# A two-layer transformer block whose layer and expert loops are written out: constant counts and addresses in place of registers and jumps

## The chip, the cores and the metric

The kernel runs on one core of one Trainium2 chip. The metric is the device time in microseconds of one execution. The kernel before takes 2094.49 us, the median of 3 runs (2094.24 to 2097.22).

## What is computed

Two layers on x of 2 sequences of 2048 tokens with 256 features, in float32. Each layer normalizes, scales and shifts x by rows made from a conditioning vector, applies a mixer, adds it back through a gate, and does the same with a feed-forward part.

- Layer 0's mixer is gated linear attention in chunks of 64 (4 heads, keys of 128, values of 64); its feed-forward part is 64 small one-input networks.
- Layer 1's mixer is a state-space scan: for 512 channels and 16 states, one step per token,

```
dtv = sigmoid(dt_t + dt_head_b)
dtv = dtv / (1 + dtv * sum(k_t * k_t))
state = state * (1 - dtv * k_t * k_t) + (x_t * dtv) * k_t
y_t = sum over the states of state * q_t
```

- Layer 1's feed-forward part is 8 experts, each of which takes the 512 tokens of a sequence that score highest for it:

```
g, m = top_k(softmax(x @ gate_w), 512)
h = gelu(x[m] @ w1[e]) @ w2[e]
out[m] += g * h
```

## The kernel before, in words

The program is written by hand: each engine (PE, DVE, ACT, POOL, and SP for the DMA queue) has its own list of instructions, and they meet at semaphores, whose counts only go up. An engine's sequencer reads the list, does register work, jumps and DMA issues itself, and hands the rest to the engine behind it.

**The layers** cut the 4096 tokens into NB = 16 blocks of 256. A block passes through five stages (A attention, F the rest up to the scan's inputs, S scan, C what comes after the scan, G gate scores), and in turn i the stages work on blocks i+2, i+1, i, i-1 and i-2. A turn is 64 steps; the table `AT` says at which step each piece is put into its engine's list. `pipeline` writes the turns: -1 to 2 written out, 3 to 13 as a loop (11 passes), 14 to 18 written out again. So turns 2 and 14 are the same Python code as the loop's body, with a constant in place of the register: turn 2 has no stage G yet, and turn 14 no longer loads a block of x. Each engine has a loop of its own and jumps back on its own; nothing joins the engines at the jump.

The scan's pieces are what the turn is full of. For each of the 16 states, SP reads that state's k and q rows back from memory, broadcast over 128 partitions, into one of 4 slots of `kqb` (`spread`, L1262 to L1264); POOL makes the input, `st = u * k` (L1090); DVE scans in place (L1071, four instructions per state) with decays that ACT makes (L1052) and PE turns (L1022); POOL reads out, `sq = st * q` (L1080), and PE adds the turned result up in PSUM (L1039). POOL's list puts the input of state m+3 between the read-outs of states m and m+1, and adds small pieces of the four layer norms (L466 to L469). A slot of `kqb` is loaded again once its state is read out:

```
sp.wait_ge(sem("read_out"), it * DS + n - SLOTS + 1)
both = kq_d[bass.ds(it % 2, 1)].rearrange("o (w n) t -> o n w t", w=2)[:, n]
sp.dma_start(kqb[:, n % SLOTS], both.broadcast_to([P, 2, TB])).then_inc(sem(f"kq_in{n % SLOTS}"), 16)
```

In a turn SP's list is: `kqb` of states 4 to 9, the output rows (L1276), the normalized rows for the experts (L1279), the next load of x (L1256), `kqb` of states 10 to 15, then for the next block the k and q rows (L1289), `ndT` (L1293) and `kqb` of states 0 to 3. DVE's list has, near its start, two halves of `ndS` (L993), scans, the gated `lz` (L769) and the two halves of `u` (L999), the scan input of the next block.

In the loop, a count such as `it * DS + n - 3` and an address such as block `it % 2` are made from the loop's register by the sequencer (a register instruction, shown by the profile as ALU_OP, FUSED_REGOPS or MOVE) ahead of the instruction that uses it. In the turns that are written out they are constants in the instruction.

**The experts** are 16 lists (8 experts, 2 sequences) after the choice of tokens. `every_turn` loops over three turns of 4 lists (2 experts) and writes the fourth out, with less in it, since nothing is prepared for a next one. Per list PE multiplies in split precision (L1750: `ph`, 8 pieces; `po`, 4 pieces), ACT applies gelu and copies, DVE splits values (L1590, L1593) and scales (L1632), POOL gathers and scatters rows; POOL's part is written out already. Two short loops stand beside it: SP loads the weights of experts 1 to 7 (L1457), and ACT copies the first expert's 8 weight pieces (L1693).

Of the kernel before, what the change touches and what calls it, by code (L numbers as in the profile page):

```python
# [19 lines left out]
NB = B * T // TB  # L20
# [10 lines left out]
E, F = 8, 1024  # L31
# [132 lines left out]
def layers(nc, sem, x_rows, consts, weights, folds, wmod0, wmod1, out_rows, xn_d,  # L164
           scores, ones_s, ident_s, col1, gb1):
    with ExitStack() as ctx:
# [1130 lines left out]
        def pipeline(eng, a_turn):  # L1297

            a_turn(eng, -1, "A")
            a_turn(eng, 0, "AF")  # L1300
            a_turn(eng, 1, "AFS")
            a_turn(eng, 2, "AFSC")
            with eng.Fori(3, NB - 2) as i:
                a_turn(eng, i, "AFSCG")
            a_turn(eng, NB - 2, "AFSCG")
            a_turn(eng, NB - 1, "FSCG")
            a_turn(eng, NB, "SCG")
            a_turn(eng, NB + 1, "CG")
            a_turn(eng, NB + 2, "G")

        with nc.Block() as block:
            @block.sync
            def _(sp):
                pipeline(sp, turn_sp)
                sp.wait_ge(sem("x_out"), (NB + 1) * 16)
                sp.wait_ge(sem("rows_out"), (NB + 1) * 16)

            @block.tensor
            def _(pe):
                pipeline(pe, turn_pe)  # L1320

            @block.scalar
            def _(act):
                act.preload_act_table_set("natural_log_exp_and_others")
                act.wait_ge(sem("tail0"), 2)
                pipeline(act, turn_act)
# [18 lines left out]
def experts(nc, sem, consts, w1_d, w2_d, out_rows, xn_d, scores, ones_s, ident_s, col1, gb1):  # L1345
    with ExitStack() as ctx:
# [16 lines left out]
        WQ = 2 * DC * F // K  # L1363
# [48 lines left out]
        def flat(x):  # L1412
            return x.rearrange("p a b -> p (a b)")
# [5 lines left out]
        ITEMS = NL // 4  # L1419
# [8 lines left out]
        def splits(i, n, ahead):  # L1428

            no_weights = WQ // 2 if n == 3 and not ahead else 0  # L1430
            return FIRST + (i - 1) * 4 * PER_LIST + n * PER_LIST - no_weights

        def ring(n, more):

            return (FIRST + n * PER_LIST + more) % 4

        def every_turn(eng, a_turn):
            with eng.Fori(1, ITEMS) as i:
                a_turn(eng, i, True)
            a_turn(eng, ITEMS, False)  # L1440

        with nc.Block() as block:
            @block.sync
            def _(sp):
                def load(e):
                    for n, w_d in enumerate((w1_d, w2_d)):
                        sp.dma_start(w_in[:, n].rearrange("p (c f) -> p c f", c=w_d.shape[1] // P),
                                     w_d[bass.ds(e, 1)].rearrange("e (c p) f -> p (e c) f", p=P))\
                            .then_inc(sem("w_in"), 16)

                for name, dst in (("bitsf", bitsf[:, :]), ("samelist", samelist[:, :]),
                                  ("segbefore", segbefore[:, :]), ("iota", iota[:, :]),
                                  ("token", token[:, :, :].rearrange("p a n -> p (a n)"))):
                    a, n = CONST_AT[name]
                    sp.dma_start(dst, consts[:, a:a + n]).then_inc(sem("const2_in"), 16)
                load(0)
                with sp.Fori(1, E) as e:  # L1457

                    sp.wait_ge(sem("w_split"), e * WQ)
                    load(e)  # L1460

            @block.vector
            def _(dve):
# [145 lines left out]
                def a_turn(dve, i, ahead):  # L1609
                    for n in range(4):  # L1610
# [34 lines left out]
                        if n % 2 == 1 and ahead:  # L1645
                            for c in range(2):
                                slots_of(i * 4 + n - 1 + c, c)

                every_turn(dve, a_turn)

            @block.scalar
            def _(act):
                act.wait_ge(sem("sel_step"), 2)
                act.activation(prob[:, :, :].rearrange("p t e -> p (t e)"), scores[:, :], ACT.Exp)\
                    .then_inc(sem("prob_exp"), 1)

                def put(to, count, at_ring):

                    act.wait_ge(sem("masked"), count)
                    act.activation(to, masked[:, at_ring, :], ACT.Copy).then_inc(sem("upper"), 1)  # L1660

                def put_weights(slot, q, count, at_ring):
                    n, at = q // 4, (q % 4) * K
                    put(w_up[:, slot, n, at:at + K], count, at_ring)

                def modulated(k_count, b):
                    for c in range(DC):
                        act.wait_ge(sem("gt_mm"), k_count + c + 1)
                        sc, sh = ((what * DC + c) * B + b for what in (4, 3))
                        act.activation(hg[:, c, :], pt[:, c, :], ACT.Identity, bias=col1[:, sh:sh + 1],  # L1670
                                       scale=col1[:, sc:sc + 1]).then_inc(sem("hg"), 1)

                def a_turn(act, i, ahead):
                    for n in range(4):
                        for f in range(FT):
                            act.wait_ge(sem("up_mm"), i * 4 * FT + n * FT + f + 1)

                            act.wait_ge(sem("h1_split"), i * 4 * FT + n * FT + f - 3)
                            act.activation(h1[:, f % 4, :], ph[:, f % 2, :], ACT.Gelu).then_inc(sem("gelu"), 1)  # L1679
                            if f > 0:  # L1680
                                put(h1_up[:, f - 1, :], splits(i, n, ahead) + f, ring(n, f - 1))
                        put(h1_up[:, FT - 1, :], splits(i, n, ahead) + FT, ring(n, FT - 1))
                        if ahead or n < 3:

                            modulated((i * 4 + n + 1) * DC, (n + 1) % 2)
                            for c in range(DC):
                                put(hg_up[:, c, :], splits(i, n, ahead) + FT + c + 1, ring(n, FT + c))
                        if ahead or n < 2:
                            for q in range(WQ // 2):
                                put_weights(1 - n // 2, n % 2 * (WQ // 2) + q, splits(i, n, ahead) + FT + DC + q + 1,  # L1690
                                            ring(n, FT + DC + q))

                with act.Fori(0, WQ) as q:  # L1693
                    act.wait_ge(sem("masked"), q + 1)
                    act.activation(flat(w_up[:, 0])[:, bass.ds(q * K, K)], flat(masked[:, :, :])[:, bass.ds(q * K, K)],
                                   ACT.Copy).then_inc(sem("upper"), 1)
                modulated(PER_TURN["gt_mm"], 0)
                for c in range(DC):
                    put(hg_up[:, c, :], WQ + c + 1, (WQ + c) % 4)
                every_turn(act, a_turn)  # L1700

            @block.tensor
            def _(pe):
# [50 lines left out]
                def a_turn(pe, i, ahead):  # L1754
                    for n in range(4):
# [24 lines left out]
                        if ahead and n % 2 == 1:  # L1780
                            for c in range(2):
                                slots_of(i * 4 + n - 1 + c, c)

                every_turn(pe, a_turn)

            @block.gpsimd
# [98 lines left out]
```

## Time and profile before

| what | value |
|---|---|
| time, median of 3 runs | 2094.49 us |
| the profiled execution's own time | 2097.58 us |
| its span, first to last instruction | 2095.4 us |
| PE busy | 1771.5 us (85%), 12344 matmuls |
| DVE busy | 1569.0 us (75%) |
| ACT busy | 1301.9 us (62%) |
| POOL busy | 1439.5 us (69%) |
| DMA | 132.78 MB, mean 63 GB/s |
| mean granted TensorE clock | 0.934 of full speed |

How to read it: times are in us from the span's first instruction. PE is the matmul part of TensorE and PEld its weight loads; DVE is VectorE, ACT ScalarE, POOL GpSimd, SP the engine that issues most DMAs. A name with q (POOLq) is the engine's sequencer, whose register work, jumps and issues are not counted as busy. A view by windows gives for each stretch its length, then busy time and instructions of each engine, the granted clock, the DMA engines' busy share and GB/s. A view of waits gives who waited for whom: us in total, times, longest. In a timeline the number in brackets is the engine's idle time just before, and what ended it; "issue" there is a time in which it waited for nothing that the profile shows. The view of one source line gives the count and then minimum, median and maximum of the duration in ns, and the first and last start.

### The profile page before, as it was taken

What the parts mean: (1) busy time and instruction counts of PE and PEld (TensorE: products, weight loads), DVE (VectorE), ACT (ScalarE), POOL (GpSimd) and SP (SyncE); (2) the same over time, 40 slices, a digit from 0 to 9 for tenths busy, and PEclk for the clock granted to TensorE, in tenths of its full rate; (3) what the DMA queues carried; (4) which work ended last, traced back from release to release, by engine and by line L of the source; (5) the groups of instructions that cost most, each with busy time, mean ns of one, the idle gap of its engine ahead of it and who ended that gap; (6) DMA issues with size and microseconds to landing.
All of it is one profiled execution on the core that took longest, in us unless ns stands there. A gap on an engine that the chain in (4) does not pass through costs nothing. (4 is left out here: it accounts for less than half of the span.)

```text
span 2095.4 us, 40115 instructions
## 1 busy us (share of the span) xinstructions
PE 1771.5 (85%) x12344; PEld 1521.1 (73%) x12344; DVE 1569.0 (75%) x3158; ACT 1301.9 (62%) x2316; POOL 1439.5 (69%) x836
## 2 busy tenths in 40 slices
PE   5578998989989899898998989988662499999996
PEld 5456887877878778787887878876551388888886
DVE  3336898887978888888888888987646777777772
ACT  0257787776867777777777777876321255555552
POOL 0005899998989989899898999999970244343342
PEclk9788999999999999999999999999875599999998
DMA  4001332223223233322322222223211233333321
GB/s 167 15 1 47 68 67 60 65 58 76 62 56 64 59 75 56 64 65 57 76 55 65 63 59 76 60 64 61 69 39 57 71 79 81 77 81 75 76 45 21
DMA packets 110368, 132.78 MB, mean 63 GB/s; under 512 B 7969, under 2 KB 103073, under 8 KB 109985
## 3 DMA queue, kind: packets, MB, share of 16 engines
q1 hardware_dynamic: 97680, 113.04, 22.3%
q0 software_dynamic: 12288, 16.79, 4.4%
q10 hardware_dynamic: 272, 1.57, 0.2%
q8 instruction: 41, 0.67, 0.1%
q14 instruction: 87, 0.70, 0.1%
HBM read 105.68 MB, written 17.30 MB: 59 GB/s over the span
## 5 line engine op out<-in xcount | busy, mean ns | idle before, releaser
L1071 DVE TENSOR_TENSOR_SCAN st<-pD,last,st 128x256 f32<-128x256 f32 x1024 | 693.9, 732 | 136.3 <-PE pD L1022 114.3
L1090 POOL TENSOR_TENSOR st<-u,kqb 128x1024 f32<-128x1024 f32 x256 | 605.0, 2363 | 85.2 <-DMA kqb<-kq_rows 76.1
L1080 POOL TENSOR_TENSOR sq<-st,kqb 128x1024 f32<-128x1024 f32 x256 | 605.0, 2363 | 26.9 <-DVE st L1071 22.5
L1052 ACT ACTIVATE decT<-ndT,ones_s,kkT 128x512 f32 (+1 forms) x512 | 407.4, 806 | 81.5 <-PE pD L1022 72.6
L1039 PE MATMUL pY<-ident_s,sq 128*128 128x128 f32 x2048 | 324.6, 283 | 62.1 <-POOL sq L1080 62.0
L1022 PE MATMUL pD<-ident_s,decT 128*128 128x128 f32 x2048 | 326.2, 284 | 53.7 <-DVE st L1071 48.3
L1022 PEld LDWEIGHTS pD<-ident_s,decT 128*128 128x128 f32 x2048 | 251.3, 146 | 108.8 <-DVE st L1071 61.6
L1039 PEld LDWEIGHTS pY<-ident_s,sq 128*128 128x128 f32 x2048 | 247.3, 145 | 81.8 <-POOL sq L1080 77.5
L1805 POOL DMA_INDIRECT y_out<-ys,ids x64 | 108.6, 1698 | 247.1 <-DVE ys L1632 150.4
L1750 PE MATMUL po<-w_up,h_up 128*128 128x256 f32 x512 | 147.8, 289 | 19.9 <-DVE h_rest L1593 19.0
L1750 PE MATMUL po<-w_rest,h_up 128*128 128x256 f32 x512 | 145.5, 284 | 0.0
L1750 PE MATMUL po<-w_up,h_rest 128*128 128x256 f32 x512 | 145.4, 284 | 0.0
L1794 POOL DMA_INDIRECT xg<-xn_rows,ids x64 | 69.3, 1083 | 91.6 <-DVE gates L1581 72.4
L1679 ACT ACTIVATE h<-ph 128x512 f32<-128x512 f32 x128 | 76.6, 598 | 76.5 <-PE ph L1750 73.5
L621 PE MATMUL pA<-hA,W 128*128 128x256 f32 x512 | 118.5, 379 | 0.8 <-DVE qg L708 0.8
L1750 PEld LDWEIGHTS po<-w_up,h_up 128*128 128x128 f32 x512 | 98.7, 193 | 25.1 <-issue 17.0
L1750 PE MATMUL ph<-hg_up,w_up 128*128 128x512 f32 x256 | 103.7, 405 | 8.9 <-DVE w_rest L1593 6.4
L466 POOL TENSOR_TENSOR nm_a<-mv_a,minus 128x2 f32<-128x2 f32 x16 | 3.1, 195 | 155.5 <-DVE ve_a L461 154.2
L621 PEld LDWEIGHTS pA<-hA,W 128*128 128x128 f32 x512 | 94.8, 190 | 19.2 <-issue 7.2
L1750 PE MATMUL ph<-hg_up,w_rest 128*128 128x512 f32 x256 | 102.7, 401 | 0.0
L1750 PE MATMUL ph<-hg_rest,w_up 128*128 128x512 f32 x256 | 102.7, 401 | 0.0
L1750 PEld LDWEIGHTS po<-w_up,h_rest 128*128 128x128 f32 x512 | 98.9, 193 | 0.0
(269 smaller groups left out, 3756.3 us busy)
## 6 DMA issues: line engine op xcount, KB each, us to landing
kqb<-kq_rows SPq DMA_DIRECT2D x256, 256.0 KB, 4.6
w_in<-w_d SPq DMA_DIRECT2D x16, 1024.0 KB
ndT<-ndS SPq DMA_DIRECT2D x16, 512.0 KB, 3.4
xt<-x_in SPq DMA_DIRECT2D x16, 256.0 KB, 2.8
y_out<-xo SPq DMA_DIRECT2D x16, 256.0 KB, 4.8
xn_rows<-xnC SPq DMA_DIRECT2D x16, 256.0 KB, 2.1
W<-weights SPq DMA_DIRECT2D x1, 3505.5 KB, 21.9
wmod<-wmod ACTq DMA_DIRECT2D x1, 1536.0 KB, 11.0
```

The costliest lines, as they stand in the source:

```text
L466: pool.tensor_tensor(nm[n][:, :], mv[n][:, :, 0], minus[:, :], ALU.mult)
L621: i = pe.matmul(bank[:, h2 * TB:(h2 + 1) * TB], wt[:, c, h * DK:(h + 1) * DK], hA[:, c, :], start=(c == 0), stop=(c == DC - 1))
L1022: i = pe.transpose(pD[h][:, k2 * TB + t * P:k2 * TB + (t + 1) * P], decT[:, m % 2, t, (2 * h + k2) * P:(2 * h + k2 + 1) * P], ident_s[:, :])
L1039: i = pe.matmul(pY[:, t, k * P:(k + 1) * P], sq[:, m % 2, k, t * P:(t + 1) * P], ident_s[:, :], start=False, stop=(m == DS - 1), is_transp ...
L1052: act.activation(decT[:, m % 2, t, :], turn2(ndT, it, NT * DI, t * DI, DI), ACT.Identity, bias=ones_s[:, 0:1], scale=turn2(kkT, it, NT * D ...
L1071: dve.tensor_tensor_scan(run, pD[h][:, k2 * TB:(k2 + 1) * TB], run, last[:, bass.ds(later(it) * (DS * DT) + m * DT + k, 1)], ALU.mult, ALU ...
L1080: pool.tensor_tensor(sq[:, m % 2], st[:, m % 4], kqb[:, m % SLOTS, 1, :].unsqueeze(1).broadcast_to([P, DT, TB]), ALU.mult).then_inc(sem("r ...
L1090: pool.tensor_tensor(st[:, m % 4], turn2(u, it, DT * TB).rearrange("p (k t) -> p k t", k=DT), kqb[:, m % SLOTS, 0, :].unsqueeze(1).broadca ...
L1679: act.activation(h1[:, f % 4, :], ph[:, f % 2, :], ACT.Gelu).then_inc(sem("gelu"), 1)
L1750: m = pe.matmul(to, stationary(c, p0), moving(c, p1), start=(n == 0), stop=(n == len(terms) - 1))
L1794: pool.indirect_dma_start(xg[:, b, s, :], None, xn_d[:, :], bass.IndirectOffsetOnAxis(ap=ids[:, k * SL + s:k * SL + s + 1], axis=0))\
L1805: pool.indirect_dma_start(out_rows, bass.IndirectOffsetOnAxis(ap=ids[:, k * SL + s:k * SL + s + 1], axis=0), ys[:, b, s, :], None, compute ...
```

## The change

Four loops over a register become Python loops, so that their bodies stand in the lists once per pass: the layers' turns 3 to 13 on all five engines, the experts' turns 1 to 3 on PE, ACT and DVE, SP's loads of expert weights 1 to 7, and ACT's 8 copies. Counts and addresses become constants, and the jumps and the register work go. The work, its order and its waits stay.

```diff
@@ -1300,7 +1300,7 @@
             a_turn(eng, 0, "AF")
             a_turn(eng, 1, "AFS")
             a_turn(eng, 2, "AFSC")
-            with eng.Fori(3, NB - 2) as i:
+            for i in range(3, NB - 2):
                 a_turn(eng, i, "AFSCG")
             a_turn(eng, NB - 2, "AFSCG")
             a_turn(eng, NB - 1, "FSCG")
@@ -1435,7 +1435,7 @@
         def every_turn(eng, a_turn):
-            with eng.Fori(1, ITEMS) as i:
+            for i in range(1, ITEMS):
                 a_turn(eng, i, True)
             a_turn(eng, ITEMS, False)
@@ -1454,7 +1454,7 @@
                 load(0)
-                with sp.Fori(1, E) as e:
+                for e in range(1, E):
 
                     sp.wait_ge(sem("w_split"), e * WQ)
                     load(e)
@@ -1690,7 +1690,7 @@
-                with act.Fori(0, WQ) as q:
+                for q in range(WQ):
                     act.wait_ge(sem("masked"), q + 1)
```

DVE's list near the start of a turn, in the loop before. ISA and REGISTER_ALU are the sequencer's register instructions; L999 makes `u`, the scan input of the next block.

```order
L768 REGISTER_ALU
L769 TENSOR_TENSOR lz<-pA,sg 128x512
L997 ISA
L998 ISA
L999 ISA
L999 TENSOR_TENSOR u<-pB,xs 128x512
L997 REGISTER_ALU
L999 ISA
```

The same place in the list of the change:

```order
L769 TENSOR_TENSOR lz<-pA,sg 128x512
L999 TENSOR_TENSOR u<-pB,xs 128x512 x2
L1071 SCALAR_TENSOR_TENSOR st<-pD,last,st 128x256 x2
L773 TENSOR_TENSOR og<-pA,lz 128x512
L453 BN_STATS stat_a<-xt 128x6 x2
```

The register instructions are gone, six in the piece shown, and the engine's own instructions stand as they stood.

SP's list in the middle of a turn, in the loop before: the two output DMAs, the load of x, and the first `kqb` load behind them.

```order
L1276 DMA y_out<-xo 128x2x256
L1279 DMA xn_rows<-xnC 128x2x256
L1282 ISA
L1256 ISA x2
L1256 DMA xt<-x_in 128x2x256
L1262 REGISTER_ALU
L1264 ISA
L1264 DMA kqb<-kq_rows 128x2x256
```

The same place in the list of the change:

```order
L1264 DMA kqb<-kq_rows 128x2x256 x10
L1276 DMA y_out<-xo 128x2x256
L1279 DMA xn_rows<-xnC 128x2x256
L1256 DMA xt<-x_in 128x2x256
L1264 DMA kqb<-kq_rows 128x2x256 x6
```

Here too only the register rows have gone: three ahead of the load of x and two ahead of each `kqb` load.

## Rows read from the trace of the kernel before

**Rows 1.** Busy time by windows, the layers (PE, PEld, DVE, ACT, POOL, clock, DMA):

```profile
150.00:1565.00 1415.00, 1264.38 (x9137) 1075.78 (x9137) 1158.88 (x2246) 1024.77 (x1843) 1256.15 (x689) 0.96 0.28 62
```

**Rows 2.** The layers' loop line: the jumps on POOL's and DVE's sequencer:

```profile
L1303 POOLq COMPARE_BRANCH  x11: 40/45/45, 401.0 to 1280.3; - x11
L1303 DVEq COMPARE_BRANCH  x11: 55/63/72, 418.5 to 1297.5; - x11
```

**Rows 3.** POOL by windows (POOL, clock, DMA): turns 3-13, turn 2, turn 14:

```profile
318.78:1284.76 965.98, 867.57 (x485) 0.98 0.29 64
232.40:318.78 86.38, 78.88 (x46) 1.00 0.28 65
1284.76:1367.72 82.96, 78.88 (x45) 1.00 0.26 65
```

**Rows 4.** POOL's waits, us 318.78 to 1284.76, the 11 looped turns:

```profile
POOL st L1090 <- DMA kqb<-kq_rows: 59.6, 54, 4.0
POOL sq L1080 <- DVE st L1071: 18.9, 20, 1.8
POOL nm_b L466 <- DVE ve_b L461: 5.2, 9, 1.4
POOL st L1090 <- issue: 3.6, 11, 0.3
```

**Rows 5.** POOL's waits, us 1284.76 to 1367.72, turn 14, written out:

```profile
POOL st L1090 <- DMA kqb<-kq_rows: 3.1, 5, 2.0
POOL sq L1080 <- DVE st L1071: 0.2, 1, 0.2
```

**Rows 6.** POOL's waits, us 232.40 to 318.78, turn 2, written out:

```profile
POOL st L1090 <- DMA kqb<-kq_rows: 2.9, 2, 2.7
POOL sq L1080 <- PE pY L1039: 2.8, 2, 1.5
```

**Rows 7.** DVE's timeline behind the jump at the end of looped turn 9:

```profile
951.49 1.39 DVE L1071 TENSOR_TENSOR_SCAN st<-pD,last,st 128x256 f32<-128x256 f32 x2 [1.51 <-PE pD L1022]
...
955.13 1.29 DVE L999 TENSOR_TENSOR u<-pB,xs 128x512 f32 x2 [1.67 <-issue]
```

**Rows 8.** DVE's timeline at the same place of turn 14, written out:

```profile
1300.88 1.39 DVE L1071 TENSOR_TENSOR_SCAN st<-pD,last,st 128x256 f32<-128x256 f32 x2 [1.00 <-PE pD L1022]
...
1302.77 1.28 DVE L999 TENSOR_TENSOR u<-pB,xs 128x512 f32<-128x512 f32 x2
```

**Rows 9.** DVE's waits, us 318.78 to 1284.76, the 11 looped turns:

```profile
DVE u L999 <- issue: 18.7, 10, 2.3
```

**Rows 10.** DMA queues, us 934.51 to 1022.19, looped turn 10 (packets, MB, share):

```profile
q14 instruction: 5, 0.04, 0.1%
```

**Rows 11.** DMA queues, us 1284.76 to 1367.72, turn 14, written out:

```profile
q8 instruction: 4, 0.07, 0.3%
q14 instruction: 3, 0.02, 0.1%
```

**Rows 12.** SP's timeline in looped turn 10:

```profile
1011.36 0.38 SPq L1279 DMA_DIRECT2D xn_rows<-xnC  x1
1012.19 0.39 SPq L1256 DMA_DIRECT2D xt<-x_in  x1
1012.84 2.45 SPq L1264 DMA_DIRECT2D kqb<-kq_rows  x2
```

**Rows 13.** SP's timeline in turn 14, written out:

```profile
1357.60 0.39 SPq L1279 DMA_DIRECT2D xn_rows<-xnC  x1
1358.03 3.43 SPq L1264 DMA_DIRECT2D kqb<-kq_rows  x2
```

**Rows 14.** Experts by windows (all engines), lists 3, 11 (looped), 13 (written out):

```profile
1715.14:1739.95 24.81, 23.64 (x152) 21.47 (x153) 17.14 (x36) 14.05 (x24) 11.21 (x8) 1.00 0.47 128
...
1927.64:1954.08 26.44, 25.27 (x152) 22.63 (x153) 17.14 (x36) 14.05 (x24) 10.75 (x8) 0.94 0.45 119
1981.48:2006.13 24.65, 23.64 (x152) 21.44 (x153) 17.19 (x36) 14.05 (x24) 11.19 (x8) 1.00 0.46 129
```

## The prediction

> **What bounds the kernel now.** I read the windows first. From us 150 to 1565, two thirds of the time, the layers run, and POOL is busy 1256 of 1415 us; PE comes near it, but its busy time is that of overlapping records, and DVE and ACT stand at 1159 and 1025 [rows 1]. So I go to POOL and cut the layers at its own beat. The start of the input of state 11 comes once per turn, and its starts cut the stretch into the looped turns 3 to 13, which take 965.98 us, or 87.82 us each, with POOL busy for 867.57/11 = 78.87 of it [rows 3]. POOL is idle 8.95 us per turn, and only that can go: its work is the same after the change.
>
> The kernel holds its own experiment: turns 2 and 14 are the loop's body written out. Turn 14 takes 82.96 us with the same 78.88 us of POOL's work, so POOL idles 4.08 us in it; turn 2 takes 86.38 us [rows 3]. The waits say where the rest goes. Per looped turn POOL waits 59.6/11 = 5.42 us for the `kqb` loads, 18.9/11 = 1.72 for DVE's scans, 5.2/11 = 0.47 for DVE's layer-norm value, and 0.33 for nothing seen, which is its own register work in front of L1090 [rows 4]. In turn 14 it waits 3.1 us for `kqb` and 0.2 for DVE [rows 5].
>
> **What DVE is late for.** After the jump DVE idles twice in a few us: 1.51 us before a scan and 1.67 us before `u`, where it waits for no semaphore that the profile shows [rows 7]. In turn 14 the same scan has 1.00 us before it and `u` nothing [rows 8]. The wait before `u` stands in 10 of the 11 looped turns, 18.7 us in all, 1.87 each [rows 9]. It is not the jump instruction, which takes DVE 63 ns [rows 2]. The DMA queues show code being read: a looped turn has five reads on q14, though it runs the code of the turn before again, and a written-out turn has three on q14 and four on q8 [rows 10, 11]. I take `u`'s wait to be code that the jump left behind and that must be read again, with DVE's list standing still. The Trainium skill ("Runtime: NRT & Kernel Launch", section Instruction fetch mechanics) says that a taken branch to a page outside the two held forces a fetch before the engine goes on, while straight code is fetched ahead; the trace agrees, with 1.87 us behind a jump and none in turn 14. By that rule alone DVE's 11 × 1.87 = 20.6 us would be the gain, if POOL followed DVE one to one.
>
> **The change, part by part.**
>
> *The layers' loop, turns 3 to 13.* The four differences of turn 14 from a looped turn are 5.42 − 3.1 = 2.3 us of `kqb` waits, 1.72 − 0.2 = 1.5 of waits for DVE, 0.47 and 0.33: together 4.6 of the 4.86 us by which the turn is shorter; the rest lies in gaps too short for the view. The first is SP's: in the loop, register instructions stand between the read-out that frees a slot and the load's issue, and such a load lands only just in time. Where SP's list is held by the two output DMAs, 1.48 us pass from the issue of the normalized rows to the next `kqb` load, two register groups and the load of x among them [rows 12], against 0.43 us in turn 14 [rows 13].
>
> Turn 14 has no load of x, though, and the turns written out will have it. By [rows 12] its issue takes 0.39 us, with some 0.05 us to the next instruction. I add 0.45 us for that, all on the longest `kqb` wait, and 0.05 for its transfer beside the load: 83.46 us per turn. Turn 2, which has the load, shows 2.7 us for that longest wait where turn 14 shows 2.0 [rows 5, 6], so the addition lies between 0 and 0.7. The saving is 87.82 − 83.46 = 4.36 us per turn, times 11 = **48.0 us**.
>
> Bounds: turn 14 as it stands gives 4.86 × 11 = 53.5 us. Turn 2 as it stands gives 1.44 × 11 = 15.8 us. I stay near turn 14: it is full like the loop's turns and follows a full turn, while turn 2's extra 2.8 us are two waits for PE's adding-up (pY) [rows 6], in the turn where stage C appears for the first time; turn 14's waits do not have them [rows 5].
>
> *The experts' loop, 12 lists.* Here PE leads. Looped list 3 takes 24.81 us and the written-out list 13 takes 24.65, with the same work [rows 14]: 0.16 × 12 = **2 us**. From below this is 0, if the little idle time moves elsewhere. Three of the 12 looped lists meet a stretch at the lower clock (1.2 GHz); in the one shown it costs 26.44 − 24.81 = 1.63 us, at clock 0.94 over the list [rows 14]. Whether they meet it after the change I leave open: up to 4.9 us more, and as much less should others meet it.
>
> *SP's loop over expert weights and ACT's over 8 pieces* I cost at nothing: ACT's copies follow DVE's splits, and the weights are loaded a whole expert ahead. If that cover were gone, it would be some register instructions of about 0.1 us, 15 times.
>
> *Added:* nothing that computes. What comes new is PE's code: looped turn 10 has no read on q8, turn 14 has four [rows 10, 11], so 11 turns bring some 44 reads. In turn 14 they are hidden behind code already there; its POOL waits contain what they cost. If they were not hidden, see the second rival.
>
> Sum: 48.0 + 2 = 50 us from the execution that was profiled, 2097.6, gives 2047.6 us. That execution stands 3.1 us above the median of the runs, so against 2094.5 the forecast is **2044.5 us**.
>
> **Rivals.**
>
> *Only the jumps and POOL's register work go.* Then DVE's waits are of another kind, say a true dependence, and stay; so do the loads' 5.42 us. What goes is 0.33 us per turn in front of L1090 [rows 4] and 0.05 us for a jump [rows 2]: 0.38 × 11 = 4 us, and 2090 us. Against it speaks that turn 14 has neither DVE's waits nor a third of the loads'. The Trainium skill ("Advanced Engine Details and Errata", Control Flow Timing) gives about 108 ns for a compare-and-branch; by that rule alone the change would be worth 11 × 0.108 = 1.2 us on POOL, an estimate from that page. The rows have 45 and 63 ns for the jump, and most of the loss stands behind it.
>
> *Reading straight-line code costs more than the jump: slower.* A written-out turn needs seven reads where a looped one needs five, and all of PE's are new [rows 10, 11]. A read that an engine has to wait for costs about 1.87 us [rows 9]. The place would be PE's list, before a scan's decays are turned, where DVE and then POOL stand behind it. It decides from 4.36/1.87 = 2.3 exposed reads per turn; with three, a turn would be 1.25 us longer, and 11 turns 14 us: 2108 us. For it: the whole list has never been read without a pause in between, and five engines would do it at once. Against it: turn 14 does exactly this, and no wait of POOL there goes back to it [rows 5]; turn 2's waits for pY are the only ones that could [rows 6]. The Trainium skill ("Advanced Engine Details and Errata", ISA Cache) has TensorE hold 128 KB of code, four times the other engines, and only two cache lines; by this rule the loop's body can stay in PE, which agrees with no q8 read in looped turn 10, and it speaks against writing out the loop.
>
> *The `kqb` chain or PE takes over.* With DVE earlier, the start of a turn would wait as in turn 2, for PE's adding-up: 15.8 + 2 = 18 us gained, 2076.5 us. For it: turn 2 is such a turn. Against: turn 14 too, and it is steadier.
>
> **How the numbers follow.** The forecast, turns at turn 14's price with or without the load of x, gets 0.82. PE taking over 0.07, no more than the jumps 0.06, slower 0.05. The low end is 53.5 + 2 + 4.9 = 60.4 us gained, 2034, and I go to 2032 for a turn that does a little better than 14 with both neighbours written out. The high end is half way between the two written-out turns: turn 14 with its load at 83.46 and turn 2 at 86.38 make 84.9, or 2.9 × 11 = 32 us, less up to 3 for the clock: 2065.5. So the range is 2032 to 2066. A measurement of this kernel can tell 0.2%, 4.2 us, from no change. The forecast and the PE rival are faster by more, 0.89; the jump rival is within it, plus the edge of the slower one, 0.06; slower 0.05.
>
> **What would show it.** Right: turns 3 to 13 at 83 to 84 us with POOL busy 78.9; `u` without its wait for nothing; `kqb` waits near 3.5 us per turn; POOL's waits for DVE under 0.5; some 40 more reads on q8; lists of the experts at 24.65 where the clock is full. Wrong: PE's or DVE's waits for nothing that the profile shows inside turns 3 to 13, which would be code; POOL waiting for pY in every turn; or turns that keep 87 us although `u` comes early.

## The result, and the profile after

| | time, us | runs | against before |
|---|---|---|---|
| before, same chip | 2095.85 | 4 (2094.24 to 2099.12) | |
| the change | 2059.6 | 4 (2057.32 to 2060.82) | 0.9824 [0.9807, 0.9841] |

The change is faster, by 36 us; 50 were forecast. The direction and the range (2032 to 2066) hold, and the predicted 2044.5 is 15 us too low. The execution that was profiled took 2060.5 us, its span 2058.7, which is 36.7 less than before. Page of the change, parts 1, 3 and 5:

```profile
span 2058.7 us, 34361 instructions
...
PE 1756.5 (85%) x12344; PEld 1512.6 (73%) x12344; DVE 1572.4 (76%) x3158; ACT 1297.1 (63%) x2314; POOL 1440.2 (70%) x836
...
q8 instruction: 98, 1.61, 0.3%
...
q14 instruction: 71, 0.58, 0.1%
...
L1090 POOL TENSOR_TENSOR st<-u,kqb 128x1024 f32<-128x1024 f32 x256 | 605.2, 2364 | 65.1 <-DMA kqb<-kq_rows 59.0
L1080 POOL TENSOR_TENSOR sq<-st,kqb 128x1024 f32<-128x1024 f32 x256 | 605.1, 2364 | 16.7 <-PE pY L1039 11.0
```

Every engine has the work it had (ACT's count in the page is two records short of the 2316 before). 5754 instructions are gone (40115 before), all of the sequencers' own. POOL's wait ahead of its scan step L1080 is now put down to PE's adding-up `pY`; in the loop it was DVE's scan. POOL cut at the same beat as before, the start of the input of state 11, for turn 2, turns 3 to 13, and turns 14 to 16 [rows 3] (columns: window, length, POOL busy, clock, DMA share, GB/s):

```profile
232.15:319.55 87.40, 78.87 (x44) 1.00 0.27 65
```

```profile
319.55:1251.76 932.21, 867.00 (x486) 0.99 0.30 67
1251.76:1503.64 251.88, 231.92 (x122) 0.92 0.32 64
```

The same for turns 14 to 16 of the kernel before:

```profile
1284.76:1531.30 246.54, 232.00 (x122) 0.93 0.28 65
```

So the 36.7 us are: turns 3 to 13 965.98 − 932.21 = 33.8 shorter, which is 84.75 us per turn and not the 83.46 forecast; turn 2 1.0 longer (86.38 before); turns 14 to 16, whose code had been written out before, 5.3 longer; and the rest, from the first of the experts' matmuls to the end, 435.4 − 426.2 = 9.2 shorter. POOL's waits in turns 3 to 13 [rows 4]:

```profile
POOL st L1090 <- DMA kqb<-kq_rows: 42.8, 35, 4.0
POOL sq L1080 <- PE pY L1039: 5.2, 10, 1.0
POOL nm_c L466 <- DVE ve_c L461: 4.8, 8, 1.3
POOL st L1090 <- PE pY L1039: 2.8, 4, 1.0
POOL sq L1080 <- DVE st L1071: 2.5, 11, 0.5
```

Per turn: 3.89 us for `kqb` (5.42 before, 3.5 forecast), 0.23 for DVE's scans (1.72 before), nothing of its own register work (0.33). New are 8.0/11 = 0.73 us for `pY`, and 0.44 for the third layer norm's value, about what the loop lost at the second. That value is DVE's too: together POOL waits 0.66 us for DVE, where under 0.5 was forecast. DVE's timeline at the place of [rows 7, 8], end of turn 9:

```profile
927.83 1.38 DVE L1071 TENSOR_TENSOR_SCAN st<-pD,last,st 128x256 f32<-128x256 f32 x2
930.34 1.39 DVE L1071 TENSOR_TENSOR_SCAN st<-pD,last,st 128x256 f32<-128x256 f32 x2 [1.12 <-PE pD L1022]
931.65 0.67 DVE L769 TENSOR_TENSOR lz<-pA,sg 128x512 f32<-128x512 f32 x1
932.23 1.28 DVE L999 TENSOR_TENSOR u<-pB,xs 128x512 f32<-128x512 f32 x2
```

`u` starts as the step before it ends; its 1.67 us are gone. The 1.12 us ahead of the scan are PE's. POOL and PE in the same us:

```profile
927.52 2.37 POOL L1090 TENSOR_TENSOR st<-u,kqb 128x1024 f32<-128x1024 f32 x1
930.88 2.36 POOL L1080 TENSOR_TENSOR sq<-st,kqb 128x1024 f32<-128x1024 f32 x1 [1.00 <-PE pY L1039]
```

```profile
926.30 0.33 PE L598 MATMUL pA<-qg,S 128*64 128x64 f32 x2
926.47 0.28 PE L600 MATMUL pA<-att,vh 128*64 128x64 f32 x2
...
928.33 0.28 PE L598 MATMUL pA<-qg,S 128*64 128x64 f32 x2
```

From 926.3 us on PE works through 64 matmuls of the attention's output without a pause. They stand in its list ahead of a scan step's `pD` and `pY`, which follow at 929.6 and 930.1, and POOL, no longer held back by DVE, arrives before them at the read-out of state 12.

Code reads, turns 3 to 13: before, and after (queue, packets, MB, share):

```profile
q14 instruction: 57, 0.47, 0.2%
q8 instruction: 6, 0.10, 0.0%
```

```profile
q8 instruction: 52, 0.85, 0.4%
q14 instruction: 39, 0.32, 0.1%
```

On q8 there are 46 reads more, as forecast (some 40); on q14 there are fewer than in the loop, which runs the same code eleven times.

Of the experts, the 12 lists that were looped take 321.44 us before and 313.80 now. The first line of each view is all 12 together, the second is list 2, one of even number. The last two lines of the view after are list 3, of odd number and at the full clock, and list 7, which meets the lower clock (1.2 GHz) for a part of it; all engines as in [rows 14]:

```profile
1660.04:1981.48 321.44, 299.30 (x2016) 268.11 (x2017) 236.60 (x428) 172.41 (x291) 123.23 (x91) 0.97 0.30 71
1687.66:1715.14 27.48, 24.93 (x187) 22.32 (x185) 22.41 (x37) 14.04 (x24) 11.03 (x8) 1.00 0.23 39
```

```profile
1632.51:1946.31 313.80, 294.84 (x2016) 265.42 (x2017) 236.82 (x428) 169.66 (x289) 125.05 (x91) 0.99 0.32 73
1659.28:1686.32 27.04, 24.88 (x187) 22.35 (x185) 22.37 (x37) 14.05 (x24) 11.14 (x8) 1.00 0.25 40
1686.32:1710.95 24.63, 23.63 (x153) 21.45 (x153) 17.18 (x36) 14.05 (x24) 11.16 (x8) 1.00 0.48 128
1789.68:1815.93 26.25, 25.25 (x152) 22.58 (x153) 17.18 (x36) 14.05 (x24) 10.71 (x8) 0.93 0.46 121
```

A list of odd number (24.81 before) lost 0.18 us and one of even number 27.48 − 27.04 = 0.44, six of each: 3.7 us. From list 2 on, two lists fewer meet 1.2 GHz, one now for three before, at some 1.6 us each [rows 14]: 3.2 us. The 0.7 us that are left of the 7.6 belong to list 1. It meets the lower clock in both kernels, a fourth one that the forecast did not count, and takes 27.61 us before and 26.77 now. The other 1.6 us of the 9.2 lie outside these lists, nearly all in the last of the 16 (40.17 us to the end before, 38.67 now), and are not the change's: after_again, the same kernel, has 40.26 there.

### The profile page after: what moved, and what is told of

Its sections match the earlier page's. It is cut to its first block and busy times, and to the rows that moved or that the text cites. A ratio compares the mean times of both kernels' runs of the same rounds, so it can differ in the third digit from the quotient of the medians.

```text
span 2058.7 us, 34361 instructions
## 1 busy us (share of the span) xinstructions
PE 1756.5 (85%) x12344; PEld 1512.6 (73%) x12344; DVE 1572.4 (76%) x3158; ACT 1297.1 (63%) x2314; POOL 1440.2 (70%) x836
## 5 line engine op out<-in xcount | busy, mean ns | idle before, releaser
L1080 POOL TENSOR_TENSOR sq<-st,kqb 128x1024 f32<-128x1024 f32 x256 | 605.1, 2364 | 16.7 <-PE pY L1039 11.0
L1052 ACT ACTIVATE decT<-ndT,ones_s,kkT 128x512 f32<-128x512 f32 x512 | 407.0, 806 | 83.1 <-PE pD L1022 69.7
L1022 PE MATMUL pD<-ident_s,decT 128*128 128x128 f32 x2048 | 323.0, 282 | 46.7 <-DVE st L1071 40.2
L1022 PEld LDWEIGHTS pD<-ident_s,decT 128*128 128x128 f32 x2048 | 247.5, 145 | 104.8 <-issue 50.0
```

The source lines that it names most:

```text
L1022: i = pe.transpose(pD[h][:, k2 * TB + t * P:k2 * TB + (t + 1) * P], decT[:, m % 2, t, (2 * h + k2) * P:(2 * h + k2 + 1) * P], ident_s[:, :])
L1052: act.activation(decT[:, m % 2, t, :], turn2(ndT, it, NT * DI, t * DI, DI), ACT.Identity, bias=ones_s[:, 0:1], scale=turn2(kkT, it, NT * D ...
L1080: pool.tensor_tensor(sq[:, m % 2], st[:, m % 4], kqb[:, m % SLOTS, 1, :].unsqueeze(1).broadcast_to([P, DT, TB]), ALU.mult).then_inc(sem("r ...
```

## The experiments

Each kernel is given by how it differs from the change. In layers_only, registers_straight, hint, dve_only, sp_only, all_but_pe and hint_sp_pool the experts' three loops are loops again, as before; their edits show only what differs in the layers. Turn times are those of turns 3 to 13, cut as above (before 87.82, the change 84.75). The median of before moved between the groups of experiments from 2092.9 to 2095.3, so each ratio is to the runs of before that stood beside it. A turn time comes from one profiled execution, a ratio from all of them.

| kernel | median, us | ratio to before | us per turn |
|---|---|---|---|
| layers_only | 2064.28 | 0.9877 [0.9848, 0.9905] | 84.44 |
| experts_only | 2087.99 | 0.9977 [0.9960, 0.9995] | 87.31 |
| registers_straight | 2082.29 | 0.9946 [0.9929, 0.9962] | 85.52 |
| hint | 2083.92 | 0.9949 [0.9931, 0.9967] | 85.59 |
| dve_only | 2078.54 | 0.9931 [0.9910, 0.9951] | 85.60 |
| sp_only | 2087.64 | 0.9973 [0.9959, 0.9987] | 86.79 |
| all_but_pe | 2058.96 | 0.9835 [0.9821, 0.9849] | 84.42 |
| hint_sp_pool | 2071.28 | 0.9881 [0.9862, 0.9900] | 84.45 |
| after_again | 2057.96 | 0.9834 [0.9818, 0.9849] | 84.29 |
| early10 | 2050.68 | 0.9791 [0.9766, 0.9816] | 84.34 |
| nd_first | 2050.67 | 0.9808 [0.9779, 0.9837] | 84.15 |
| both | 2044.12 | 0.9765 [0.9745, 0.9785] | 84.08 |

### The two parts of the change alone

layers_only has the experts' loops back, experts_only the layers' loop; the edit is that of experts_only:

```diff
-            for i in range(3, NB - 2):
+            with eng.Fori(3, NB - 2) as i:
                 a_turn(eng, i, "AFSCG")
```

> Only the layers' loop (turns 3 to 13) is written out; the experts' turns, SP's weight loop and ACT's copies stay loops. In the changed kernel the layers up to the first expert product are 27.5 us shorter (1660.0 to 1632.5) and the experts 9.2 us shorter. Theory A (the two parts add): 2094.5 - 27.5 = about 2068 us. Theory B (the experts' 9 us are an accident of where the clock falls, or come from the layers): 2059 to 2061 us.

> The layers' loop stays a loop; the experts' turns 1 to 3, SP's weight loop and ACT's copies are written out. Theory A: lists 2, 4 and so on go from 27.5 to 27.0 us and the odd ones from 24.8 to 24.6, which is 12 x 0.3 = 3.6 us, and the rest of the 9 us is that fewer lists meet the lower clock: 2086 to 2091 us, depending on the clock. Theory B (nothing of it comes from this loop): 2094 to 2097 us.

The median of before beside them is 2094.38. The layers alone give 30 us by medians (26 by the ratio), the experts alone 6 (5). By medians that is together the change's 36; by the ratios it is 31, with intervals of 6 and 4 us to either side. In layers_only a turn takes 84.44 us and POOL's waits are those of the change. In experts_only a turn keeps 87.31 us and `u` its wait (18.4 us in all); its even lists take 27.05 us, its odd ones 24.64, and one of the twelve 26.27. The experts' term is real, and larger than the 2 us forecast.

experts_only is also a second look at the looped layers, whose code it has unchanged. Window and longest wait of POOL in its turns 3 to 13:

```profile
320.57:1280.98 960.41, 867.67 (x486) 0.98 0.28 64
```

```profile
POOL st L1090 <- DMA kqb<-kq_rows: 47.4, 33, 4.4
POOL sq L1080 <- DVE st L1071: 20.2, 21, 2.0
```

The waits for DVE repeat (18.9 before). Those for `kqb` do not: 47.4 us instead of 59.6, and the turn is 0.5 us shorter. The profile of before is of an execution 2 to 5 us above its medians (2097.58). So what a turn saves against 87.82 can be 0.5 us too large, and a fall of `kqb` waits by 12 us in all is within what one profile differs from the next.

### Is it the jump, the code behind it, or the registers?

registers_straight keeps register addresses in turns 3 to 12 but never jumps back: each turn is a loop of a single pass.

```diff
-            for i in range(3, NB - 2):
-                a_turn(eng, i, "AFSCG")
+            for turn in range(3, NB - 3):
+                with eng.Fori(turn, turn + 2, 2) as i:
+                    a_turn(eng, i, "AFSCG")
+            a_turn(eng, NB - 3, "AFSCG")
```

hint keeps the loop, its jumps and its registers whole, and only tells the sequencers ahead of time that the jump goes back:

```diff
-            for i in range(3, NB - 2):
+            with nc.Fori(3, NB - 2, engines=bass.OrderedEngineSet([eng.engine]), hint_back_edge=True) as i:
                 a_turn(eng, i, "AFSCG")
```

> As the kernel before, but turns 3 to 12 stand in the lists ten times, each in a loop of a single pass over a register: the register work stays (somewhat less of it in turns 3 to 7, where some counts fold), no jump back is taken, no code is read twice; turn 13 is written out plainly, and the experts are those of before. Theory A (code read again behind the jump is the loss of the layers): DVE's idle time before u is gone and this takes about what layers_only takes, 2068 to 2072 us. Theory B (register work on SP, POOL and DVE is the loss): it stays near 2090 us.

> The kernel before with a prefetch hint for the jump target at the head of each pass of the layers' loop on all five engines; one more instruction per pass, register work and jump stay. Theory A (DVE stands still because the code behind the jump must be read first): DVE's 1.87 us before u go or shrink and the time falls to 2070 to 2080 us. Theory B (DVE's stall is register work or a dependence): no change, 2093 to 2097 us. If the hint covers only the first block behind the jump, DVE's first stall goes and the second stays: 2080 to 2090 us.

Both bring a turn to some 85.5 us and `u`'s wait to nothing. So 2.2 to 2.3 us of a looped turn (1.7 to 1.8 against the 87.31 of experts_only) are the code behind the jump, and neither the jump (hint has all of them) nor the registers (both have them). Code reads and POOL's waits of hint in turns 3 to 13:

```profile
q8 instruction: 5, 0.08, 0.0%
q14 instruction: 4, 0.03, 0.0%
```

```profile
POOL st L1090 <- DMA kqb<-kq_rows: 49.4, 38, 4.0
...
POOL st L1090 <- issue: 3.0, 9, 0.3
POOL sq L1080 <- DVE st L1071: 2.8, 11, 0.3
```

Where the plain loop reads 57 pieces of code on q14, this one reads 4. The waits for DVE fall from 18.9 to 2.8 us; those for `kqb`, at 49.4, are no less than in experts_only. What remains against the change, 85.59 − 84.75 = 0.8 us (1.3 against after_again, below), is left for the registers; registers_straight against layers_only, which reread no code either, gives 85.52 − 84.44 = 1.1 us. The hint is wrong once, when the loop ends, and that turn pays. POOL's window of hint's turn 14, and DVE's wait in it:

```profile
1262.25:1350.62 88.37, 78.88 (x46) 0.94 0.27 61
```

```profile
DVE ve_b L461 <- issue: 4.9, 1, 4.9
```

The whole times fall short of what was expected where rereading is the loss: 2082.29 for 2068 to 2072, and 2083.92 for 2070 to 2080. hint's eleven turns are 24.5 us shorter, but its profiled execution only 10.7. Turns 14 to 16 take 5.3 us more, the stretch from there to the experts' first product 5.5 (134.2 for 128.8), and the rest is before turn 3 and in the experts. Only turn 14's part has a cause seen here.

### Which engine's loop costs it?

In dve_only DVE alone is written out, in sp_only SP alone, in all_but_pe all but PE; the tuple names them.

```diff
-            for i in range(3, NB - 2):
-                a_turn(eng, i, "AFSCG")
+            if a_turn in (turn_dve,):
+                for i in range(3, NB - 2):
+                    a_turn(eng, i, "AFSCG")
+            else:
+                with eng.Fori(3, NB - 2) as i:
+                    a_turn(eng, i, "AFSCG")
```

> As the kernel before, but DVE's list alone has turns 3 to 13 written out; PE, ACT, POOL and SP keep the loop. Theory A (the code read again matters on DVE alone, register work on SP for the rest): a turn goes from 87.8 to about 85.6 us, as with the hint, and the time to 2070 to 2078 us. Theory B (all engines' jumps share the loss): 87 us per turn and 2085 us or more.

> As the kernel before, but SP's list alone has turns 3 to 13 written out. Theory A (SP's register work is most of what the written-out kernel saves beyond the code reads, 85.5 to 84.6 us per turn): a turn is 0.8 to 1.3 us shorter, waits for kqb fall from 5.4 to about 4.5 us per turn, and the time is 2080 to 2086 us. Theory B (SP is hidden behind DVE's lateness): 87.5 to 87.9 us per turn and 2092 to 2096 us.

> As layers_only, but PE keeps the layers' loop, so its code is not read again in turns 3 to 13 (no reads on q8 there), and its register work stays. Theory A (reading PE's straight-line code costs nothing, its register work next to nothing): as layers_only, 84.4 to 85 us per turn and 2062 to 2068 us. Theory B (the reads on q8 disturb PE or the kqb loads and cause POOL's waits for pY): a turn is 0.5 to 1.2 us shorter than in layers_only, 2052 to 2059 us. Theory C (PE's register work and jump hurt): longer by as much.

dve_only saves 2.2 us per turn, as much as hint does for all engines: the whole loss to code read again is DVE's. sp_only saves 1.0 (0.5 against experts_only). `kqb` falls by 17.8 us (5.6 against experts_only) while POOL's wait for DVE's scans stays, as does most of DVE's own before `u` (14.2 us):

```profile
POOL st L1090 <- DMA kqb<-kq_rows: 41.8, 26, 3.8
POOL sq L1080 <- DVE st L1071: 18.4, 23, 1.7
```

dve_only has it the other way round, with 49.8 us of `kqb` waits and 2.6 for DVE's scans. The two together, 2.22 + 1.03 = 3.25, lie between the 3.07 and 3.52 us that the change and its repeat save. By the ratios the whole kernels gain less than the turns: 14 us for 24 in dve_only, 6 for 11 in sp_only.

all_but_pe should be compared with layers_only, which has the experts' loops too. Its turns take 84.42 us with PE looped, against 84.44, and it reads 6 pieces on q8 where the change reads 52; POOL waits 5.0 us for `pY` in them, against 5.4. So in these turns the 46 reads of PE's straight-line code cost nothing that can be seen, and neither do PE's jump and registers. The whole time does not settle it. 2058.96 us lies in the range that was expected if the reads hurt (2052 to 2059), and not in the other (2062 to 2068). By the ratios, 0.9835 and 0.9877, the kernel with PE looped is 9 us faster than layers_only, with intervals of 3 and 6 us to either side, in different groups; and it equals after_again (0.9834, side by side), which has the experts written out as well. What these microseconds are isn't known.

hint_sp_pool writes out SP and POOL and leaves PE, ACT and DVE in the hinted loop:

```diff
+            if a_turn in (turn_sp, turn_pool):
+                for i in range(3, NB - 2):
+                    a_turn(eng, i, "AFSCG")
+            else:
+                with nc.Fori(3, NB - 2, engines=bass.OrderedEngineSet([eng.engine]), hint_back_edge=True) as i:
+                    a_turn(eng, i, "AFSCG")
```

> Turns 3 to 13: SP's and POOL's lists written out, PE, ACT and DVE in a loop with the prefetch hint. Theory A (a looped turn loses 2.2 us to code read again and about 1 us to the register work of SP, and nothing else): 84.4 to 84.9 us per turn, as in the changed kernel, though PE, ACT and DVE keep all their register work. Theory B (the register work of PE, ACT and DVE counts too): 85.2 us or more. The time should be 2070 to 2076 us, since the run with the hint alone lost some 5 us again in turn 14, right behind the loop's end, and the experts are those of before.

84.45 us per turn: the written-out turn's price with three engines looping. Against hint this is 1.1 us less, for SP's and POOL's register work, which were not parted from each other here. A looped turn's loss is then complete to the half microsecond that profiles differ by: some 2 us of code on DVE, some 1 us of register work on SP and POOL, nothing seen on PE and ACT. As a whole this kernel is some 10 us slower than after_again, by the ratios. The experts' loops are some 5 of them, and its turn 14, behind the loop's end, takes 86.5 us for 84.3, with a stall of DVE of 2.9 us at the place where hint has its 4.9.

### Why not 83.46 us per turn?

after_again is the change once more, for a second profile.

> The changed kernel once more, beside the others on the same chip: 2057 to 2061 us. Its second profile tells whether a written-out turn at 84.8 us (not 83.5) and list times of 27.0 and 24.6 us stand, and how far one turn of one profile can be off: turns 3 to 16 should again lie between 81 and 87 us, with turns 8 and 11 among the longest.

```profile
319.06:1246.28 927.22, 866.69 (x485) 1.00 0.30 67
1246.28:1495.41 249.13, 231.86 (x121) 0.91 0.28 65
```

The same kernel, 5 us shorter in these eleven turns: 84.29 us each. Over both profiles the 22 turns lie between about 83 and 87 us. Most of this spread repeats by place: turn 8 takes 86.17 and 86.05 us in the two profiles, turn 12 82.98 and 82.93. Turn 14 of the kernel before, at 82.96, stands at the short end, and this repeats too: behind looped layers it takes 83.16 us in experts_only and 83.43 in sp_only. After the change turn 14 itself takes 84.9 and 84.3 us, though its code is unchanged. So it was short by its place, behind the looped turns, and no price for the others; what makes a place long or short was not tried.

What the turns wait for was tried from two sides. early10 moves the `kqb` load with the longest wait, that of state 10, ahead of the output of the normalized rows in SP's list (the later loop then begins at 11):

```diff
                              xo[:, :, :]).then_inc(sem("x_out"), 16)
+                if s is not None:
+                    for n in range(10, 11):
+                        spread(s, n)
                 sp.wait_ge(sem("lnd_rows"), c + 1)
...
             if s is not None:
-                for n in range(10, DS):
+                for n in range(10 if c is None else 11, DS):
                     spread(s, n)
```

nd_first issues the load of `ndT` ahead of the wait for the rows of `kq`:

```diff
                 sp.wait_ge(sem("ndt"), f + 1)
-                sp.wait_ge(sem("kq_out"), f * 16 + 16)
                 sp.dma_start(turn2(ndT, f, NT * DI), flat(ndS[:, :, :])).then_inc(sem("nd_in"), 16)
+                sp.wait_ge(sem("kq_out"), f * 16 + 16)
```

> The changed kernel, with the kqb load of state 10 issued between the two output DMAs, ahead of the wait for the normalized rows, in place of behind them and the load of x. Theory A (the longest kqb wait, 3.0 us per turn before the input of state 10, is only SP's list standing behind that wait): it falls under 0.5 us, a turn goes from 84.6 to 82.0 or so, and the time from 2059.6 to 2020 to 2030 us. Theory B (PE and DVE are nearly late already, so they take the wait over): the wait goes, others grow, 2045 to 2055 us. Theory C (the load itself is slow there): no change.

> The changed kernel, with ndT issued before SP waits for the k and q rows to have landed, about 4 us earlier in every turn. Theory A (in written-out turns ACT, then PE and DVE, start the next block late because ndT lands late, which is POOL's wait for pY and for the third layer norm's value, together 1.2 us per turn that turn 14 of the kernel before did not have): these waits go, a turn takes 83.5 us and the time is 2045 to 2050 us. Theory B (PE is late for another reason, its code or its clock): 2057 to 2062 us.

> The changed kernel with both moves in SP's list: the kqb load of state 10 ahead of the wait for the normalized rows, and ndT ahead of the wait for the k and q rows. Each alone took about 9 us off. Theory A (they act on different waits and add): 2040 to 2043 us. Theory B (both end in the same wait for PE's bursts): 2047 to 2051 us.

In early10 the wait of state 10, 3.0 us per turn in the change, is gone. The turn is not 3 us shorter, it takes 84.34 us. POOL's waits in turns 3 to 13:

```profile
POOL sq L1080 <- PE pY L1039: 22.3, 21, 1.5
POOL sq L1080 <- DVE st L1071: 17.2, 25, 1.9
POOL st L1090 <- DMA kqb<-kq_rows: 9.4, 19, 1.0
```

`kqb` gave up 33.4 us of waiting, and PE and DVE took nearly all of it: `pY` stands at 22.3 instead of 8.0 and DVE's scans at 17.2 instead of 2.5. They come at the read-outs of states 9, 10 and 12; the one at state 12 (11.9 us for `pY`) is right behind the burst shown above. The load and PE's and DVE's own lateness hold POOL at nearly the same time; take one away and the others are the end. This is what was expected if PE and DVE are nearly late already (2045 to 2055 us). The whole kernel still gains, some 9 us against after_again by the ratios; 3.8 of them are turn 2, which takes 83.6 us instead of 87.4.

In nd_first ACT's waits for nothing seen ahead of L1052, which I read as waits for `ndT` (2.28 us the longest in the change), are gone and a turn takes 84.15 us, 0.1 to 0.6 less than the change in its two profiles. POOL's waits for `pY` ahead of L1080 stayed, 5.0 us in all against 5.2, so a late `ndT` isn't their cause. The time, 2050.67 us, fits neither expectation: the waits stayed, and yet the kernel gains 5 us against after_again by the ratios. both has 84.08 us per turn and 2044.12 us in all. It is the fastest kernel here, 0.9765 of before: some 14 us against after_again, which ran beside it, and 9 + 5 are 14. With intervals of 3 to 6 us on each of these ratios the two gains add as far as can be told; the time lies between the two ranges expected.

## Why the prediction was right, and where it was not

**What bounds the kernel: right.** POOL's work is the same to 0.6 us over eleven turns, and only its idle time changed, from 8.95 to 5.93 us per turn.

**What DVE is late for: right, and now shown.** It was argued from turn 14 that `u`'s wait is code read again. hint has the jumps and the registers and not the wait; registers_straight and dve_only agree. The wait repeats in experts_only, 18.4 us. The Trainium skill's rule ("Runtime: NRT & Kernel Launch", section Instruction fetch mechanics), that a taken branch out of the held pages stops the engine for a fetch, agrees with these runs; by that rule alone the gain was to be 20.6 us (ten stalls and not eleven, 18.7 us in all [rows 9]). DVE's part measured 2.22 × 11 = 24.4 us of turns, or 1.71 × 11 = 18.8 with experts_only for the loop; POOL follows DVE about one to one.

**The loads' waits: right in kind.** SP's register work is one cause: with SP alone written out they are 41.8 us, and 59.6 and 47.4 in the two profiles with SP looped. Behind the normalized rows the next `kqb` load is issued after 0.92 us in nine of eleven turns, near the 0.88 reckoned from [rows 12, 13]. The size was wrong, below.

**The layers' term, 4.36 us per turn: mis-sized, and this is the step that failed.** It measured 3.07 and 3.52 in two profiles, 33.8 and 38.8 us for 48.0. The forecast took turn 14 of the kernel before as the price of a written-out turn. One turn was no fair sample where turns differ by 4 us and by place. Its `kqb` wait of 2.0 us plus 0.45 for the load of x was to be the longest wait of a turn; measured is 3.0, near turn 2's 2.7 [rows 6], which I had in hand as the other end. That wait, ahead of the input of state 10, was 3.2 us in the loop, so it hardly moved; what shrank are the `kqb` waits at the other states, from 24 to 10 us in all (12 in the loop of experts_only). And the terms did not simply vanish: 0.73 us for `pY` (1.03 in after_again) and 0.44 for the third layer norm's value came in. That POOL meets such waits when it arrives earlier is shown by early10, where those for `pY` grow as the loads' waits shrink; the layer norm's does not grow there (3.1 us for 4.8), and its cause is open. Why turn 14 was short, and what part of that its missing load of x has, was not separated.

**What the sum left out: the neighbours.** Turn 2 and turns 14 to 16 stand in the sum with nothing; their code does not change. They got longer by 1.0 and 5.3 us (2.6 in after_again). The loss is read, not explained: a single profile of turns that vary this much doesn't settle it. It means that the gain in the layers is 27.5 us (35 in after_again) and not what the eleven turns show.

**The experts' term, 2 us: too small.** The pair of lists compared, 3 and 13 [rows 14], were both of odd number, where 0.18 us goes. The even-numbered lists lose 0.44. 12 × 0.16 = 2 should have been 6 × 0.18 + 6 × 0.44 = 3.7. The even list was not read. PE's waits for DVE's `h_rest` fall from 14.2 to 12.0 us over the 12 lists, which is the largest piece seen; what delays DVE there was not tried by itself. The clock added 3.2 of the up to 4.9 us that the forecast had left open: from list 2 on, two lists fewer met 1.2 GHz. That is not shown to be the change's doing; after_again and experts_only have one such list of these eleven too, but so has all_but_pe, whose experts are looped.

**Small loops, and PE's code: nothing seen, as forecast.** The small loops were not tried by themselves. For PE's code the prediction named a sign: PE waiting for nothing that the profile shows. Its weight loads do so in turns 3 to 13, in the change and, ahead of L1022, less before:

```profile
PEld pD L1022 <- issue: 40.2, 58, 2.3
PEld pA L538 <- issue: 18.4, 17, 1.6
```

```profile
PEld pD L1022 <- issue: 17.7, 46, 0.8
PEld pA L538 <- ACT hA L489: 16.8, 11, 1.5
```

I read these as dependences under another name and not as code. The matmuls themselves wait there for DVE's scan and ACT's `hA`, the weight loads of L538 waited for `hA` before, and no read on q8 starts in these waits or in the 3 us ahead of any of the 22 that are over 1 us. all_but_pe has none over 1 us, and its turns are not shorter.

**The rivals.** "Only the jumps": excluded, the jump is worth nothing that can be measured and what stands behind it some 2 us. "Straight-line reads exposed, slower": excluded as it was put, since the kernel is faster; in the turns all_but_pe shows no cost of PE's reads, while its whole time leaves room for one of some microseconds elsewhere. DVE waits for nothing seen only 0.3 us at a time, and ACT's five such waits of up to 2.3 us (one in after_again) were most likely for `ndT`, since nd_first has none. The Trainium skill's ISA Cache rule ("Advanced Engine Details and Errata"), that TensorE holds 128 KB of code, agrees with the reads on q8, 6 in eleven turns while PE loops and 52 written out, but the turns' time doesn't show it. "PE takes over": a part of it came true. The turns did not fall back to turn 2's 86.4, but POOL waits for `pY` in them as it did in turn 2, and the high end of the range, laid half way between turns 14 and 2 at 84.9 us, is close to the 84.75 measured. The layers' term was too high, and the experts' and the clock's too low; that the total stayed inside the range owes something to these partly making up for each other.

## What to carry to other kernels

In this kernel a loop cost what DVE had to read again behind the jump, and what register work put ahead of a late DMA issue, and only on the engines that set the pace. So try writing out those lists first and leave the others looped (all_but_pe is as fast with PE's loop kept; DVE's and SP's lists alone, both written out, were not tried). A hint for the jump gives the same turns as writing out DVE, but gives back a part where the loop ends. When a kernel holds a sample of its changed form, price from all of its samples and from a repeat of the profile, not from the best one; the kernel before needs the repeat as much. Idle time that has several near-equal causes returns little when one is removed: here 33.4 us of waits for one load turned into 29 us of waits for two engines.

## What the runs showed of the hardware

- The branch hint cut the code reads of eleven looped turns from 57 to 4 on q14 and removed DVE's stall; at the loop's end, where it guesses wrong, DVE stood still once for 4.9 us (2.9 in hint_sp_pool). A loop with a hint whose last pass isn't hinted was not tried.
- Of the 57 reads on q14, 20 are left when DVE alone is written out (dve_only). The change has 39.
- The jump itself takes DVE 63 ns [rows 2]. The stall behind it is 18.7/11 = 1.70 us per turn as DVE's wait shows it [rows 9], and 1.7 to 2.2 us per turn as POOL's turns pay it.
- Two profiles of one kernel differ by 7.5 us in when the layers end (1632.5 and 1625.0), while the whole runs agree within 0.3%. Two profiles of the same looped layers differ by 12 us in what POOL waits for `kqb` (59.6 and 47.4).
- Moving PE's burst of 64 matmuls, behind which POOL waits once the loads are early, was not tried. Nor were early10 and nd_first on the looped kernel, whose price is therefore only known on top of the change.
